# The product of unit 5 on VectorE in every second group of a fused Mamba and MoE layer

## The reference, cut to what matters

```
dA  = exp(delta[..., None] * A)                      # 512 channels x 16 states
dBu = delta[..., None] * Bm[:, :, None, :] * xc[..., None]
def step(h, inp):
    dA_t, dBu_t, C_t = inp
    h = dA_t * h + dBu_t
    return (h, jnp.einsum('bdn,bn->bd', h, C_t))
y = ys + xc * D
return y * silu(z) @ W_out
```

## Time and profile before

| | |
|---|---|
| time, median of 3 runs | 1708.54 us (1707.23 to 1710.84) |
| the profiled execution | 1710.15 us, span 1708.0 us |
| VectorE busy | 1544.3 us, 90% of the span |
| GpSimd busy | 1563.2 us, 92% |
| TensorE busy | 1483.6 us, 87% |
| ScalarE busy | 1328.5 us, 78% |
| mean granted TensorE clock | 0.949 of full speed |

### The profile page before, as it was taken

How to read it: one execution, slowest core, us unless ns; L and a number is a source line. 1 busy time by engine, 2 the same in 40 slices (tenths; PEclk the granted TensorE clock), 3 DMA queues, 4 the chain that set the end, 5 groups by cost and what they waited for, 6 DMA issues and landing times.

```text
span 1708.0 us, 28038 instructions
## 1 busy us (share of the span) xinstructions
PE 1483.6 (87%) x9868; PEld 1065.3 (62%) x9868; DVE 1544.3 (90%) x1389; ACT 1328.5 (78%) x3100; POOL 1563.2 (92%) x782
## 2 busy tenths in 40 slices
PE   8778898899889988898888898988988889896688
PEld 7656666666666666666666666666666666664355
DVE  2499999999999999999999999999999999999944
ACT  2577788888888888888888888888888888887644
POOL 0599999999999999999999999999999999999914
PEclk8888999999999999999999999999999999997899
DMA  4667755566667555666665556666655566566110
GB/s 136 143 126 178 182 127 124 121 133 140 136 137 152 125 124 117 137 142 138 135 153 125 121 120 137 142 137 136 153 125 122 123 133 142 121 143 140 39 35 16
DMA packets 194430, 218.47 MB, mean 128 GB/s; under 512 B 94011, under 2 KB 184773, under 8 KB 193778
## 3 DMA queue, kind: packets, MB, share of 16 engines
q1 hardware_dynamic: 193522, 215.51, 56.9%
q0 software_dynamic: 576, 1.17, 0.3%
q10 hardware_dynamic: 192, 0.01, 0.0%
HBM read 169.92 MB, written 47.09 MB: 127 GB/s over the span
## 4 chain that ended last, share of the span: by engine, by line
DVE 24%; POOL 19%; ACT 18%; issue 13%; PE 12%; DMA 12%; SPq 2%; DVEq 0%; ACTq 0%; POOLq 0%
DVE psum L1317 12%; POOL xr L1664 12%; ACT psum L1020 7%; DMA u<-u_scratch 7%; DVE xr L1317 5%; DVE xr L1326 5%; PE psum L620 4%; DMA u_scratch<-u 4%; POOL u L1685 3%; ACT L1142 2%; POOL xr L1672 2%; ACT L1051 2%; PE psum L792 2%; SPq L482 2%; ACT soft L1068 2%
## 5 line engine op out<-in xcount | busy, mean ns | idle before, releaser
L1664 POOL TENSOR_TENSOR xr<-u,bbc 128x912 f32<-128x912 f32 x512 | 1076.3, 2137 | 13.7 <-DMA u<-u_scratch 13.7
L1020 ACT ACTIVATE psum<-delta,a_neg 128x228 f32<-128x228 f32 x2048 | 804.9, 440 | 199.4 <-DVE xr L1326 159.3
L1317 DVE TENSOR_TENSOR_SCAN psum<-psum,xr 128x912 f32<-128x912 f32 x320 | 654.3, 2045 | 10.6 <-POOL xr L1664 7.4
L1672 POOL TENSOR_TENSOR xr<-xr,cbc 128x912 f32<-128x912 f32 x192 | 409.3, 2132 | 35.7 <-DVE xr L1317 32.7
L1317 DVE TENSOR_TENSOR_SCAN xr<-psum,xr 128x912 f32<-128x912 f32 x192 | 393.3, 2048 | 31.3 <-ACT psum L1020 31.3
L1326 DVE TENSOR_TENSOR xr<-psum,cbc 128x912 f32<-128x912 f32 x320 | 352.2, 1101 | 3.8
L721 PE MATMUL psum<-xr,fold 128*32 128x228 f32 x4096 | 294.7, 385 | 30.3 <-POOL xr L1672 16.6
L620 PE MATMUL psum<-xh,win 128*128 128x228 f32 x1024 | 222.9, 367 | 41.0 <-ACT xs L1051 31.6
L620 PEld LDWEIGHTS psum<-xh,win 128*128 128x128 f32 x1024 | 192.6, 193 | 68.4 <-ACT xs L1051 41.9
L671 PE MATMUL psum<-xi,conv_d 128*128 128x228 f32 x1024 | 211.2, 358 | 0.0
L671 PEld LDWEIGHTS psum<-xi,conv_d 128*128 128x128 f32 x1024 | 190.5, 189 | 16.3 <-issue 11.7
(11 more groups left out here) (204 smaller groups left out, 1590.4 us busy)
## 6 DMA issues: line engine op xcount, KB each, us to landing
delta<-delta_scratch SPq DMA_DIRECT2D x256, 228.0 KB, 6.6
u<-u_scratch SPq DMA_DIRECT2D x256, 228.0 KB, 4.4
bbc<-bc_scratch SPq DMA_DIRECT2D x128, 114.0 KB, 2.6
u_scratch<-u SPq DMA_DIRECT2D x64, 228.0 KB, 4.1
cbc<-bc_scratch SPq DMA_DIRECT2D x128, 114.0 KB, 2.8
delta_scratch<-delta SPq DMA_DIRECT2D x64, 226.0 KB, 6.3
out<-ob SPq DMA_DIRECT2D x32, 228.0 KB
h_scratch<-h SPq DMA_DIRECT2D x31, 228.0 KB
```

The source lines that it names most:

```text
L1020: ins = nc.scalar.activation(slot(k)[:, j * TOK:(j + 1) * TOK], delta4[:, c // 2, j, c % 2], ACT.Exp, scale=a_neg[:, c, j, n:n + 1])
L1317: nc.vector.tensor_tensor_scan(x if k in on_pool(i) else slot(k), slot(k), x, 0.0, ALU.mult, ALU.add).then_inc(scan_done, 1)
L1664: nc.gpsimd.tensor_tensor(xr[:, k % XRING], u4[:, c // 2, :, c % 2], bbc[:, p, n].unsqueeze(1).to_broadcast([P, J, TOK]), ALU.mult).then_i ...
L1672: nc.gpsimd.tensor_tensor(xr[:, k % XRING], xr[:, k % XRING], cbc[:, p, k % NI].unsqueeze(1).to_broadcast([P, J, TOK]), ALU.mult).then_inc ...
```

## The change

`ON_POOL` gets a second entry, so the groups alternate: even groups (0, 2, ...) as before, odd groups (1, 3, ..., 31) without unit 5. In these the scan of unit 5 writes its PSUM slot, VectorE and not GpSimd multiplies it with C, and the exponentials of unit 7, which reuse the slot, wait for that product and not for the scan. TensorE waits for VectorE's product at unit 5. All counts that the waits use follow from `on_pool`.

```diff
-ON_POOL = ((2, 5, 8, 10, 12, 14),)
+ON_POOL = ((2, 5, 8, 10, 12, 14), (2, 8, 10, 12, 14))
```

## The result

The changed kernel takes 1715.78 us (median of 6 runs, 1714.84 to 1717.56) against 1708.32 (median of 6, 1707.23 to 1710.84) for the kernel before: a ratio of 1.0033, 95% interval 1.0018 to 1.0048. That is 5.6 us by the ratio and 7.5 by the medians, slower and clear of no change. The profiled execution took 1717.39 us with a span of 1715.6, 7.6 more than before's span.

A forecast was written before the change was run, and what follows sets the result against it. VectorE's queue and its three waits for ScalarE or TensorE were taken to set the pace; 6.3 (14 odd groups) + 1.1 (group 1) + 0.2 (group 31) = 7.6 us, on 1708.54 giving 1716.1, range 1711.5 to 1722.5 us.

The forecast's parts named there:

- The product adds 1.12 us: VectorE behind scan 5 of odd groups: one more product lengthens its queue by 1.12 us, 17.9 over 16 groups if nothing absorbs it.
- 0.67 us of it is taken in at delta_out, 0.45 is left: Ordinary odd groups: VectorE's 0.67 us wait ahead of delta_out absorbs part of the 1.12, leaving 0.45 each.
- The exponentials of unit 7 don't spoil it: ScalarE: waiting for the new product, they start at 715.87 instead of 715.31 and move the Abs by only some 0.05 us.
- rival (a): At delta_out: its chain starts behind the new product, nothing is absorbed, each odd group costs 1.12, +17.9, 1726.4 us; chance 0.08.
- Nothing is taken in at the next group's start: Waits ahead of y_out (0.4) and scan 2 (0.9) stay unchanged, as their chain starts from VectorE's own product 15.
- rival (b): Next group's start: waits of 0.4 and 0.9 us absorb the 0.45; only groups 1 and 31 pay, +1.4, 1709.9 us; chance 0.09.
- GpSimd's relief gives nothing: GpSimd in odd groups: the saved 2.13 us product turns into waiting, 1.0 us ahead of u, 0.9 ahead of product 8; gain 0.
- Rival (d): Shared SBUF port: the new VectorE product is held up by the GpSimd instruction beside it, +25, 1733 us; chance 0.02.
- Group 1: No v_norm and no wait at delta_out there, so the added product costs its 1.12 us in full.
- Groups 2 to 29: The 14 ordinary odd groups, 3 to 29, cost 0.45 us each, 6.3 us in all.
- behind scan 2 of group 31: Group 31 has no delta_out, but scan 7's 0.88 us wait for its exponentials absorbs part of 1.12, leaving 0.24.
- off the path with 0.77 us to spare: GpSimd waits 0.77 us a group for VectorE's scan of unit 2 and follows it; VectorE hardly ever waits for GpSimd.

The follow-up runs named there:

- drop5: Kernel before with product 5 of the odd groups left out altogether, so GpSimd has less work and VectorE gets nothing: ratio 1.0000 (0.9991 to 1.0009).
- all5: Kernel before with unit 5 given to VectorE in all groups, not only the odd ones: ratio 1.0075 (1.0062 to 1.0089).
- swap7odd: Kernel before with, in odd groups, unit 5 given to VectorE and unit 7 to GpSimd: ratio 1.0146 (1.0128 to 1.0164).

## Why the prediction was right

Its range held the time and its mechanism is the one that the experiments found. The sizes, step by step:

- *The product adds 1.12 us.* Measured in group 13: scan 5 to product 2.10, product to scan 6 1.02, less the 1.97 that was there: 1.15.
- *0.67 us of it is taken in at delta_out, 0.45 is left.* v_norm to delta_out was 8.09 us and is 8.49: 0.40 left. The wait was worth 0.76 and not 0.67. Scan 7 to delta_out took 2.73 (717.71 to 720.44) and takes 1.97 (719.79 to 721.76), as delta_out, where it needn't wait, starts 0.08 us ahead of the recorded end of scan 7 (719.79 + 2.05 = 721.84). The shown idle time leaves that out.
- *The exponentials of unit 7 don't spoil it.* They start at 716.80, 3.53 us behind v_norm's start where it was 2.96, 0.57 later (0.56 was forecast), and the Abs keeps its distance to v_norm, 5.06 against 5.07 us, but the 0.54 us of idle ahead of it are used up. This was the closest call in the sum, and rival (a) hung on it.
- *Nothing is taken in at the next group's start.* The waits there are 0.38 and 0.89 in nearly all groups: rival (b) falls, and (a) with it, as an odd period is 49.19 and not 49.9.
- *GpSimd's relief gives nothing.* It waits 1.15 and 0.80 us at the two places named (1.0 and 0.9 forecast) and 1.31 ahead of the next product 2 (1.3 forecast), and drop5 gives 1.0000.
- *Rival (d).* VectorE's products take 1.100 us on average with 336 of them as with 320: no sharing.

Against before's trace the 7.6 us of the span divide thus. Until delta_out of group 0: -2.2 us, ahead of the change's first effect; drop5, which is the same there, reaches it 2.2 us before before's trace too, so it isn't the change's. Group 1: 48.66 against 47.50, +1.2 (forecast 1.1). Groups 2 to 29: +5.7 (forecast 6.3), 14 odd groups at 0.41, while stray losses in either trace cancel. Group 30: 52.36 against 50.51, +1.85, not forecast. From there to the end: +1.0, of which 0.3 comes behind scan 2 of group 31 (forecast 0.2) and 0.7 is y_out at its start, 1.56 us against 0.86; drop5 waits 1.56 there too, so this isn't the change's. That the sum hits 7.6 is chance: an unforecast gain of 2.2 us and unforecast losses of 2.6 cancel, and in the timed runs neither need be the same. By the ratio these give 5.6 us, by the medians 7.5; the mechanism as measured accounts for 1.2 + 5.7 + 0.3 = 7.2.

Group 30 is TensorE's clock. proj_delta and delta_out, before:

```profile
1546.88 1.77 PE L707 MATMUL psum<-dbl,wdt 17*128 17x228 f32 x8 [0.78 <-ACT ob L1132]
...
1551.76 1.11 DVE L1367 SCALAR_TENSOR_TENSOR delta<-psum,soft 128x912 f32<-128x912 f32 x1 [1.47 <-ACT soft L1076]
```

and after:

```profile
1551.87 3.37 PE L707 MATMUL psum<-dbl,wdt 17*128 17x228 f32 x8 [0.78 <-ACT ob L1132]
...
1558.34 1.11 DVE L1367 SCALAR_TENSOR_TENSOR delta<-psum,soft 128x912 f32<-128x912 f32 x1 [3.06 <-ACT soft L1076]
```

The same eight matmuls take 3.37 us instead of 1.77, at a granted clock of 0.50 against 1.00, the lower of the two levels against the upper, and delta comes late. The last step of ffn_out ahead of them takes 1.06 us against 0.78; the two together are about the 1.85 us. In drop5, whose VectorE queue is that of before, they take 3.37 as well and group 30 lasts 52.09 us, while in all5 it is 1.77 and 50.48. Of the 14 kept traces nine have the slow proj_delta in group 30 and five the fast one. So this loss goes with neither unit 5 nor its place. With one trace for each kernel it can't be told whether it goes with the kernel or with the single execution.

The prediction had one thing too simple, though it did no harm there. It called GpSimd off the path with 0.77 us to spare. That holds at unit 2 and for taking work away. swap7odd shows that the same engine with the same load, its work at another place, costs 1.5%, by making TensorE late and then slow.

## What to carry to other kernels

Price an edit on the engine that sets the pace by the next wait behind it, and ask where the chain that ends that wait starts: work put between the start and the end of that chain is partly free (0.4 us paid of 1.15 here), work ahead of the start or behind the end is not (1.2 and 1.4). An engine on which the bound engine never waits can still reach it through a third one that works in order: before giving it work, look at each of its results against the moment at which its reader comes to it, not at its average room. If the third one is TensorE, look at the granted clock behind its wait as well: it can cost more than the wait. And where a time grows by less than the work added, take the wait from starts of instructions, not from the idle time shown.

## What the hardware showed that I had not expected

A scan of 128 x 912 followed by an instruction that doesn't need its result takes a step of 1.97 us, followed by its own product 2.07 to 2.10 us (714.62 to 716.69 in the earlier trace rows, 713.56 to 715.66 after): 0.10 to 0.13 us for the dependence.

TensorE's granted clock fell behind waits of about 2 us for another engine's product: in nine of 14 groups of swap7odd the convolve behind such a wait took 4.4 to 5.0 us and not 3.35, in the other five 3.35. In the last stage of the loop it differs from one trace to another without a reason in the edited part: 0.91 over group 30 before, 0.86 after and in drop5, and the slow proj_delta and ffn_out there are worth 1.6 to 1.9 us.
